# The end of a graph and feed-forward network kernel: last unit in two passes, the turning before it moved ahead, and the output stored in more and smaller parts

## The reference

```python
x = x + gnn(layernorm(x), edges, W, b)
h = layernorm(x) @ lin0_w + lin0_b
h = silu(h @ swi1_w1 + b1) * (h @ swi1_w2 + b2)
h = moe(h)                                     # 8 experts, top 4, and a shared expert
h = h @ lin1_w + lin1_b
h = silu(h @ swi2_w1 + swi2_b1) * (h @ swi2_w2 + swi2_b2)
x = x + h                                      # the output, 625 x 1024
```

## Time and profile before

| what | us |
|---|---|
| median of 3 executions | 1656.29 |
| lowest and highest | 1655.44, 1656.95 |
| the profiled execution | 1656.63 |
| its span, first to last instruction | 1655.0 |
| TensorE busy in the span | 1606.2 (97%) |
| granted TensorE clock, mean over the span | 0.987 of full |

### The profile page before, as it was taken

The page is one execution under the profiler, slowest core; times in us unless marked ns, Lnnn a source line. Parts: engine busy times, 40 slices in busy tenths (PEclk is TensorE's granted clock), DMA queues, the critical chain, the costliest instruction groups (busy, mean ns, idle before and its releaser), DMA issues.

```text
span 1655.0 us, 28056 instructions
## 1 busy us (share of the span) xinstructions
PE 1606.2 (97%) x11047; PEld 1588.0 (96%) x11047; DVE 491.9 (30%) x898; ACT 520.2 (31%) x745; POOL 783.8 (47%) x396
## 2 busy tenths in 40 slices
PE   6889989999999999999999999999999899999997
PEld 5789889999999999999999999999999899999997
DVE  5865621111541011414132242424221044111011
ACT  4312123222222234334444434444444222222120
POOL 1211023332352465766767586767677566333330
PEclk8999999999999999999999999999999999999999
DMA  4301032223232254645555464646465566233220
GB/s 128 125 27 39 1 126 77 77 68 126 73 99 77 87 152 130 205 141 183 155 176 170 147 202 140 209 141 209 152 185 156 154 180 181 77 104 111 71 74 34
DMA packets 64355, 205.62 MB, mean 124 GB/s; under 512 B 13228, under 2 KB 14478, under 8 KB 64248
## 3 DMA queue, kind: packets, MB, share of 16 engines
q1 hardware_dynamic: 44718, 157.88, 32.1%
q0 software_dynamic: 14976, 32.81, 6.4%
q10 hardware_dynamic: 4554, 13.32, 2.2%
HBM read 185.01 MB, written 18.95 MB: 123 GB/s over the span
## 4 chain that ended last, share of the span: by engine, by line
PE 91%; DVE 3%; issue 2%; DMA 1%; POOL 1%; ACT 1%; SPq 0%; POOLq 0%; DVEq 0%; ACTq 0%
PE acc L1323 84%; PE acc L1298 2%; DMA rows<-x_dram 1%; PE acc L1603 1%; PE acc L1582 1%; POOL gath L436 1%; POOL w_lo L392 1%; PE acc L1370 0%; DVE yrow L769 0%; DVE gath L801 0%; PE acc L1438 0%; DVE gath L795 0%; DVE gath L793 0%; PE acc L1651 0%; PE acc L1468 0%
## 5 line engine op out<-in xcount | busy, mean ns | idle before, releaser
L392 POOL TENSOR_TENSOR w_lo<-raw,w_hi 128x1024 fp32r<-128x1024 f32 x296 | 713.6, 2419 | 761.6 <-ACT w_hi L384 756.0
L1323 PE MATMUL acc<-act_b,w_hi 128*128 128x314 f32 (+8 forms) x2560 | 518.6, 311 | 0.0
L1323 PE MATMUL acc<-act_x,w_hi 128*128 128x344 f32 (+7 forms) x2048 | 451.7, 309 | 2.3 <-POOL w_lo L392 1.7
L1323 PEld LDWEIGHTS acc<-act_b,w_hi 128*128 128x128 f32 x2560 | 409.9, 189 | 0.0
L1323 PE MATMUL acc<-act_a,w_hi 128*128 128x314 f32 x1792 | 353.3, 314 | 11.3 <-issue 5.4
L1323 PEld LDWEIGHTS acc<-act_x,w_hi 128*128 128x128 f32 x2048 | 342.3, 188 | 3.9 <-issue 3.2
L1323 PE MATMUL acc<-act_b,w_lo 128*128 128x314 f32 (+8 forms) x1280 | 332.1, 308 | 0.0
L384 ACT ACTIVATE w_hi<-raw 128x1024 fp32r<-128x1024 f32 x296 | 310.7, 1050 | 46.2 <-PE acc L1323 34.8
L1323 PE MATMUL acc<-act_x,w_lo 128*128 128x344 f32 (+7 forms) x1024 | 316.3, 309 | 0.0
L1323 PEld LDWEIGHTS acc<-act_a,w_hi 128*128 128x128 f32 x1792 | 288.6, 193 | 12.2 <-issue 5.6
L1323 PEld LDWEIGHTS acc<-act_b,w_lo 128*128 128x128 f32 x1280 | 225.1, 189 | 0.0
(11 more groups left out here) (189 smaller groups left out, 884.1 us busy)
## 6 DMA issues: line engine op xcount, KB each, us to landing
raw<-stream_dram SPq DMA_DIRECT2D x296, 512.0 KB, 3.7
y_dram<-yrow POOLq DMA_DIRECT2D x16, 512.0 KB
rows<-x_dram ACTq DMA_DIRECT2D x2, 2500.0 KB
y_dram<-yrow POOLq DMA_DIRECT2D x8, 352.0 KB
rows<-x_dram SPq DMA_DIRECT2D x5, 500.0 KB
x_dram<-rows ACTq DMA_DIRECT2D x1, 2500.0 KB
h_rows_dram<-rows ACTq DMA_DIRECT2D x1, 2500.0 KB
out_dram<-rows ACTq DMA_DIRECT2D x1, 1250.0 KB
```

What stands on the lines that cost most here:

```text
L392: nc.gpsimd.tensor_tensor(w_lo[:, s, :], raw[:, s, :], w_hi[:, s, :].bitcast(f32), ALU.subtract).then_inc(lo_split, 1)
L1323: ins = pe.matmul(o, w, xs_[h], start=(first and w is hi and xs_ is x_hi), stop=(last and w is lo))
```

## The change

On TensorE, the last pair is no longer done by `gated`: the turning of block 6 stands between unit 14 and unit 15, not behind unit 15. Unit 15 is computed with two `half_unit` calls, first for tokens 0 to 313 into bank 2, then for tokens 314 to 627 into bank 3. After the first a new semaphore, `last_half`, lets VectorE make the first half of the last product. At k = 4 of the second pass TensorE turns token blocks 0 and 1 into bank 6; behind it, blocks 2 to 4 into bank 7. VectorE adds the first two in one instruction and the last three in one.

On ScalarE's queue, each store is cut into rows 0 to 111 and rows 112 to 124 (`spread` is 112), and the columns 768 to 1023 go out in three steps: 768 to 895 after block 6's rows, 896 to 1023 of token blocks 0 and 1, and 896 to 1023 of blocks 2 to 4. There are ten output DMAs instead of three.

```diff
--- before.py
+++ after.py
@@ -293,6 +293,7 @@
         sum_used = sem("sum_used")
         o_tp = sem("o_tp")
         o_rows = sem("o_rows")
+        last_half = sem("last_half")
 
 
         ov_iota = yr.bitcast(f16)[:, 2 * D:2 * D + OV_ALL]
@@ -734,17 +735,28 @@
                 act.activation(a_hi[:, m, :], prod[:, m % 2, :], ACT.Copy).then_inc(shb_dhi, 1)
             act.dma_start(rows[0:TT, :, :], x1_dram.rearrange("(i p) d -> p i d", p=TT)).then_inc(x1_back, 16)
             linear_hi(lin1, b_hi, B_LIN1)
+            out_rows = out.rearrange("(i p) d -> p i d", p=TT)
+            spread = TT // 16 * 16
+
+            def store(i0, i1, c0, c1):
+                for r0, r1 in ((0, spread), (spread, TT)):
+                    act.dma_start(out_rows[r0:r1, i0:i1, c0:c1], rows[r0:r1, i0:i1, c0:c1]).then_inc(out_saved, 16)
+
             for m in range(KC):
                 gated_pair(swi2, m, None, B_S2A)
-                if m in (4, 6):
-                    c0, c1 = (0, 4 * P) if m == 4 else (4 * P, 6 * P)
-                    act.wait_ge(o_rows, c1 // P)
-                    act.dma_start(out.rearrange("(i p) d -> p i d", p=TT)[:, :, c0:c1],
-                                  rows[0:TT, :, c0:c1]).then_inc(out_saved, 16)
-            act.wait_ge(o_rows, KC)
-            act.dma_start(out.rearrange("(i p) d -> p i d", p=TT)[:, :, 6 * P:D],
-                          rows[0:TT, :, 6 * P:D]).then_inc(out_saved, 16)
-            act.wait_ge(out_saved, 48)
+                if m == 4:
+                    act.wait_ge(o_rows, 4)
+                    store(0, NT, 0, 4 * P)
+                if m == 6:
+                    act.wait_ge(o_rows, 6)
+                    store(0, NT, 4 * P, 6 * P)
+            act.wait_ge(o_rows, 7)
+            store(0, NT, 6 * P, 7 * P)
+            act.wait_ge(o_rows, 8)
+            store(0, 2, 7 * P, D)
+            act.wait_ge(o_rows, 9)
+            store(2, NT, 7 * P, D)
+            act.wait_ge(out_saved, 5 * 32)
             act.wait_ge(x1_saved, 16)
 
 
@@ -1272,11 +1284,31 @@
                 r = rows[0:TT, 4, m * P:(m + 1) * P]
                 dve.tensor_tensor(r, tp_tokens(m % 2, 4), r, ALU.add).then_inc(o_rows, 1)
 
-            for m in range(KC):
+            for m in range(KC - 1):
                 gated_pair(swi2, m, None, None, B_S2B, o_tp)
                 if m >= 1:
                     out_rows(m - 1)
-            out_rows(KC - 1)
+            out_rows(KC - 2)
+
+            def last_product(h):
+                n = slice(h * HT, (h + 1) * HT)
+                dve.scalar_tensor_tensor(out=prod[:, 1, n], in0=acc[:, 2 + h, 0:HT], scalar=bias[:, B_S2B, KC - 1:KC],
+                                         in1=silu[:, n], op0=ALU.add, op1=ALU.mult).then_inc(swi2.prod, 1)
+
+            def last_rows(h, i0, i1):
+                dve.wait_ge(o_tp, KC + h)
+                r = rows[0:TT, i0:i1, D - P:D]
+                dve.tensor_tensor(r, acc[0:TT, 6 + h, 0:(i1 - i0) * P].rearrange("p (i d) -> p i d", d=P), r,
+                                  ALU.add).then_inc(o_rows, 1)
+
+            dve.wait_ge(swi2.silu, KC)
+            dve.wait_ge(o_tp, KC - 2)
+            dve.wait_ge(last_half, 1)
+            last_product(0)
+            last_rows(0, 0, 2)
+            dve.wait_ge(unit_done, UNITS)
+            last_product(1)
+            last_rows(1, 2, NT)
 
 
         @block.tensor
@@ -1717,9 +1749,36 @@
                     pe.wait_ge(o_rows, m - 1)
                 to_rows(prod[:, m % 2, :], m % 2, o_tp)
 
-            gated(swi2, b_hi, b_lo, both(lin1.hi, lin1.lo), lambda m: o_turn(m - 1) if m >= 1 else None,
-                  lambda: pe.wait_ge(lin1.lo, KC - 1))
-            o_turn(KC - 1)
+            for m in range(KC - 1):
+                if m >= 1:
+                    pe.wait_ge(swi2.silu, m)
+                else:
+                    pe.wait_ge(lin1.lo, KC - 1)
+                dense(U_SWI2, 2 * m, b_hi, b_lo, both(lin1.hi, lin1.lo) if m == 0 else None)
+                if m >= 1:
+                    pe.wait_ge(swi2.prod, m)
+                dense(U_SWI2, 2 * m + 1, b_hi, b_lo)
+                if m >= 1:
+                    o_turn(m - 1)
+
+            def last_turn(h, i0, i1):
+                pe.wait_ge(swi2.prod, KC + h)
+                for i in range(i0, i1):
+                    last = pe.transpose(acc[0:TT, 6 + h, (i - i0) * P:(i - i0 + 1) * P],
+                                        prod[:, 1, i * TT:(i + 1) * TT], ident[:, :])
+                last.then_inc(o_tp, 1)
+
+            def first_tiles(k):
+                if k == 4:
+                    pe.wait_ge(o_rows, KC - 2)
+                    last_turn(0, 0, 2)
+
+            pe.wait_ge(swi2.silu, KC - 1)
+            dense(U_SWI2, 2 * KC - 2, b_hi, b_lo)
+            o_turn(KC - 2)
+            half_unit(U_SWI2, 2 * KC - 1, b_hi, b_lo, 2, 0).then_inc(last_half, 1)
+            half_unit(U_SWI2, 2 * KC - 1, b_hi, b_lo, 3, 1, first_tiles).then_inc(unit_done, 1)
+            last_turn(1, 2, NT)
 
 
 # ---- launch: weights cut into units of [128 inputs, 8 chunks, 128 outputs] ----
```

## The result

The changed kernel takes 1652.45 us (median of 9 executions, 1651.17 to 1653.06), the kernel before 1656.95 us (9 executions, 1655.44 to 1658.29). The ratio is 0.9974, 95% interval 0.9965 to 0.9984: 4.5 us or 0.26% faster. The forecast was 1651.1 with a range of 1650.2 to 1653.2. Two executions of the study stand far apart, 6206.91 us of e8_uneven_passes and 1748.9 us of the kernel before beside the last three runs; no ratio counts them, and without the first the median of e8 is 1651.5 instead of the 1651.83 of the table.

The account below looks back on a forecast made before the run. TensorE bounds the kernel, and after the last store's issue 7.26 us pass without computing. Chain -0.2 and bytes -5.0 give -5.2: execution 1651.4, set to 1651.1 us for the runs' median; range 1650.2 to 1653.2.

Parts of the forecast that it names:

- Turning ahead: TensorE: block 6's five turnings, free behind the last matmul, delay it when put ahead of unit 15: +0.47 us.
- early turnings: TensorE, second pass of unit 15: two turnings put in at k = 4, 0.094 us each, +0.19 us.
- Two passes at no cost: TensorE, unit 15: still 48 matmuls at about the same pace, so 0 us, at worst 0.1.
- third rival: TensorE waits at k = 4 for the half product, or passes leave gaps: gain 2.6 us, 1653.7; chance 0.09.
- Chain behind the last matmul: VectorE and TensorE to the last issue: product 0.55, three turnings 0.62, addition 0.55, plus gaps; issue 0.2 us sooner.
- Lead 0.86 and end 0.8: Last store: 0.86 us from issue to first bytes and 0.8 from last bytes to the span's end, as before.
- Bytes: Last store's flow: 24 pieces of 512 B per engine at 25.8 ns, 0.62 us; bounds 0.47 to 1.07.
- Sixteen and thirteen engines: Output stores: 112 rows go over 16 engines and 13 rows over 13, where 125 rows had five.
- fourth rival: Output stores: block count also limits the engines, so 112 rows get one: slower, 1706 us; chance 0.04.
- One after the other: Last stores: the 13 rows start only when the 112 have landed: gain 3.5 us, 1652.8; chance 0.07.
- The issues: ScalarE: seven more store issues at 0.27 to 0.30 us count 0; one held 8.36 us would still leave 4 us gain.
- first rival: Output stores: 112 rows keep to five engines, 75 pieces instead of 24: gain 3.9 us, 1652.4; chance 0.08.

Follow-up runs that it names:

- e8_uneven_passes: Changed kernel with the last unit in passes of 376 and 256 columns, three token blocks turned inside the second: 1651.83 us, ratio 0.9971.
- e5: Kernel before with only the turning of block 6 moved ahead of unit 15: last store issued at 17.26 us after unit 14's start, against 16.73; one execution.
- e11: Changed kernel without the very last store (rows 112 to 124, columns 896 to 1023, blocks 2 to 4): tail 2.6 us, one execution.
- e3: Changed kernel with each store's 125 rows in one DMA, not cut at row 112: 1653.75 us, ratio 0.9983, tail 3.8 us.
- e1: Kernel before with its three stores each cut into rows 0 to 111 and 112 to 124, nothing else changed: 1653.41 us, ratio 0.998.
- e7: Changed kernel with the rows of the stores cut at 100, not 112: tail 3.2 us, one execution.

## Why the prediction was right, point by point

- *What bounds it.* The 7.26 us behind the last issue were the right place. The gain in the profiles from unit 14 on is 4.8 us, of which 4.65 in the tail.
- *Turning ahead, +0.47; early turnings, +0.19.* e5 shows 0.52 for the first, and the last matmul ends 0.72 later against 0.66.
- *Two passes at no cost.* 5.22 + 1.75 = 6.97 us for 48 matmuls, 6.99 before them. Right. The cover, counted at 1.2 us, was 1.06 and held; the third rival (missed cover) falls.
- *Chain behind the last matmul, 1.86.* It took 1.84. The product of 314 columns, bounded from 0.44 to 0.55, took 0.55: the value at the fixed-part end. Issue 0.15 sooner instead of 0.2.
- *Lead 0.86 and end 0.8.* They measured 0.84 and 0.8, the end being unchanged although 16 engines close instead of five.
- *Bytes, 0.62.* This is the mis-sized term: 1.0 us. The price of a piece was drawn as a line through 2 KB and 1 KB, from the length of the flow; the busy time per packet is 85.7 (24.1% of 16 engines for 14 us over 630), 47.3 and about 30 ns, so the line falls short at 512 B by 4 ns; drawn through the busy times it would give 28 and fall short by 2. (By its own 82.8 and 44.6 it gives 25.5, not 25.8, which moves nothing.) Closing packets were left out: thirteen engines have 26 packets and three have 22, 25.25 on average, not 24. Together 0.77. The remaining 0.2 is the uneven start and end, a term that the sum did not have. The bound of 1.07 held it, but that bound was a price of 1 KB pieces and not a reason for a flow of 1.0 us.
- *Sixteen and thirteen engines.* The closing packets show both. The first and the fourth rival (five engines, one engine) fall. The rule of the Trainium skill, "DMA: Bandwidth & Descriptors", section "Why a DMA increments its semaphore by 16 and not by 1", agrees with the 5, 16 + 13 and 10 + 5 closing packets of these runs.
- *One after the other.* One burst, and leaving the second store out changes nothing (e11). The "Don't bother — they serialize" of the Trainium skill, same page, section "Rules for kernel authors", is said of two halves that both use all 16 engines, and it does not hold against this use: the two stores overlap, and the cut at 112 rows brought 1.2 us in the tail (3.8 in e3 to 2.6), since without it the 125 rows had five engines.
- *The issues.* Counted at 0.27 to 0.30, they took 0.33 for 112 rows and 0.45 to 0.49 for 13; nothing waited for the difference. An issue can be held, as the prediction feared, but the one seen (e8, 1.91 us) had 14 pieces per engine in front, far below the 100 and 125 in front of the two that were held in the earlier trace rows. Pieces in front, the reason given there, don't explain this one.
- *The level.* The forecast lies 1.35 us below the median. 0.66 of it is the level of before, 1656.29 over three executions and 1656.95 over nine; 0.7 is the gain, 4.5 against 5.2. The 1652.45 lies just outside the narrow range of the sum, 1650.3 to 1652.4, and right at the 1652.4 of the first rival, five engines for 112 rows. So the time alone would not have told the two apart, and that it fell inside the stated range owes something to a range drawn over two rivals. The closing packets, the share near 1.0 and e1 decide for the forecast's mechanism.

## What to carry to other kernels

Read the end of a kernel from the last issue: lead, bytes and end are three terms, and only the bytes changed here, by fewer bytes behind the last matmul and by a row count that more engines share; each alone gave about 3 us here, both 4.5. Count the closing packets to see how many engines a transfer uses, and for a short flow take a piece's price from the busy share over the packets: the length divided by the pieces gave 40 ns for a piece of 30. Work moved off a gap that was free comes back as cost: here it was 0.5 us, paid for because with the passes it let 192 KB be stored last instead of 640.

## What the runs showed that I had not expected

- Large pieces get dearer with more engines, small ones hardly: 2 KB 85.7 ns on five engines and 100 on 16; 1 KB 47.3 and 54; 512 B 29.3 and 30.4. The 100 are from the first output store of the changed kernel, its queue from 1601 to 1611:

```profile
q10 hardware_dynamic: 654, 1.28, 40.9%
```

- The time until unit 14 differs by up to 2.8 us between profiles of kernels whose computing code is the same up to there (1629.5 to 1632.3); between two whole spans it hides any edit at the end that is worth less.
- The second of two issues in a row takes longer than the first: 13 rows 0.45 to 0.49 us behind 112 rows with 0.33. Part of it is the place and not the rows: from SyncE the 13 rows took 0.39, and five engines took 0.40 as the second issue of e7 (25 rows) and 0.27 alone in e3 (125 rows).
